# One fused Mamba block with an expert-choice feed-forward on one core: B and C are projected and split in the first stage, one product with C a batch goes to GpSimd, TensorE adds the skip term, and the feed-forward runs one unit earlier

## The reference

```
# attn: a selective scan
delta, Bmat, Cmat = split(xn @ W_deltaBC.T, [64, 80])      # 64 + 16 + 16 columns
delta  = softplus(delta @ W_dt.T + b_dt)                   # [b, 512, 256]
deltaA = exp(delta[..., None] * -exp(A_log))               # [b, 512, 256, 16]
BX     = delta[..., None] * Bmat[:, :, None, :] * xn[..., None]
h_t    = deltaA_t * h_(t-1) + BX_t                         # scan over the 512 tokens
y      = einsum('blds,bls->bld', h, Cmat) + D * xn
# ffn: 8 experts, each takes its 128 best tokens of every batch
G, I = top_k(softmax(xn @ Wg.T over experts), 128)
out  = G * (gelu(xn[I] @ W1 + b1) @ W2 + b2)               # 256 -> 1024 -> 256
ffn  = scatter-add of out at I
```

## Time and profile before

| | |
|---|---|
| median of 3 runs | 2486.82 us |
| the profiled execution | 2487.14 us, of which the span of the trace is 2485.3 us |
| TensorE products busy | 2352.3 us, 95% |
| VectorE busy | 2420.4 us, 97% |
| ScalarE busy | 1971.0 us, 79% |
| GpSimd busy | 2200.9 us, 89% |
| DMA | 325.38 MB, mean 131 GB/s |

### The profile page before, as it was taken

How to read it: one execution, slowest core, us unless ns; L and a number is a source line. 1 busy time by engine, 2 the same in 40 slices (tenths; PEclk the granted TensorE clock), 3 DMA queues, 4 the chain that set the end, 5 groups by cost and what they waited for, 6 DMA issues and landing times. The chain is left out here.

```text
span 2485.3 us, 32917 instructions
## 1 busy us (share of the span) xinstructions
PE 2352.3 (95%) x10524; PEld 1773.3 (71%) x10524; DVE 2420.4 (97%) x2090; ACT 1971.0 (79%) x3432; POOL 2200.9 (89%) x1260
## 2 busy tenths in 40 slices
PE   7829999999999999999999999999999999999996
PEld 3307777777777777777777777777777777777775
DVE  7889999999999999999999999999999999999995
ACT  6627888888888888888888888888888888888783
POOL 4317999999989999999999999999999999999996
PEclk9959999999999999999999999999999999999998
DMA  9762464535444444454545353444544445454433
GB/s 344 254 255 79 129 182 126 145 96 130 118 116 134 116 125 109 116 134 100 151 101 149 91 143 99 132 117 117 135 115 125 110 115 132 100 151 93 106 92 54
DMA packets 162973, 325.38 MB, mean 131 GB/s; under 512 B 16272, under 2 KB 133104, under 8 KB 146160
## 3 DMA queue, kind: packets, MB, share of 16 engines
q1 hardware_dynamic: 95536, 239.11, 28.1%
q0 software_dynamic: 66048, 83.92, 20.2%
q10 hardware_dynamic: 1216, 0.23, 0.0%
HBM read 250.84 MB, written 84.93 MB: 135 GB/s over the span
## 5 line engine op out<-in xcount | busy, mean ns | idle before, releaser
L499 POOL TENSOR_TENSOR ysum<-ysum,prod 128x1024 f32<-128x1024 f32 x480 | 1306.5, 2722 | 32.7 <-DVE prod L909 23.0
L900 DVE TENSOR_TENSOR_SCAN bank_x<-decay,bank_x 128x1024 f32<-128x1024 f32 x512 | 1169.6, 2284 | 0.0
L1106 PE MATMUL bank_l<-ext,w_sb 128*128 128x256 f32 x4096 | 970.2, 382 | 4.3 <-ACT og L693 4.2
L1125 PE MATMUL bank_l<-w_sb,hid 128*128 128x256 f32 x4096 | 957.2, 383 | 0.0
L1125 PEld LDWEIGHTS bank_l<-w_sb,hid 128*128 128x128 f32 x4096 | 762.5, 190 | 164.0 <-issue 67.7
L1106 PEld LDWEIGHTS bank_l<-ext,w_sb 128*128 128x128 f32 x4096 | 756.5, 190 | 141.5 <-issue 23.5
L643 ACT ACTIVATE hid<-bank_l,b_all 128x256 f32<-128x256 f32 x1024 | 431.0, 475 | 339.6 <-PE bank_l L1106 339.1
L634 ACT ACTIVATE decay<-delta,a_sb 128x511 f32<-128x511 f32 x1024 | 640.7, 707 | 4.8 <-POOL delta L462 3.5
L909 DVE TENSOR_TENSOR prod<-bank_x,c_all 128x1024 f32<-128x1024 f32 x512 | 623.0, 1217 | 0.1
L847 DVE TENSOR_TENSOR bank_x<-du,bank_b 128x1024 f32<-128x1024 f32 x512 | 615.7, 1203 | 0.0
L518 POOL DMA_INDIRECT out<-og,idx_all x256 | 408.6, 1596 | 49.4 <-POOL ysum L499 34.5
(11 more groups left out here) (95 smaller groups left out, 1545.9 us busy)
## 6 DMA issues: line engine op xcount, KB each, us to landing
c_all<-c_rows SPq DMA_DIRECT2D x128, 1024.0 KB, 5.4
w_sb<-in_w SPq DMA_DIRECT2D x32, 1024.0 KB, 7.4
decay<-in_x SPq DMA_DIRECT2D x32, 512.0 KB, 6.3
xn_rows<-c_all SPq DMA_DIRECT2D x32, 512.0 KB, 4.9
out<-yrow POOLq DMA_DIRECT2D x32, 512.0 KB, 7.0
xr<-xn_rows SPq DMA_DIRECT2D x30, 512.0 KB, 6.6
ex<-xn_rows,idx_all POOLq DMA_INDIRECT x256, 2.8
out<-og,idx_all POOLq DMA_INDIRECT x256, 4.9
```

Source lines behind the costliest of these rows:

```text
L499: nc.gpsimd.tensor_tensor(ysum[:, m % 2], first, prod[:, i], ALU.add).then_inc(sum_done, 1)
L900: nc.vector.tensor_tensor_scan(bank_x[:, s % 2], decay[:, k % 2, i].rearrange("p c t -> p (c t)"), bank_x[:, s % 2], 0.0, ALU.mult, ALU.ad ...
L1106: i = nc.tensor.matmul(bank_l[(q + k) % 2][:, (f % 2) * UT:(f % 2 + 1) * UT], w1_sb[:, e2, hc, f * P:(f + 1) * P], ext[:, k % 2, hc], star ...
L1125: i = nc.tensor.matmul(o, hid[:, (k - 1) % 2, f, c * K:(c + 1) * K], w2_sb[:, le2, f], start=False, stop=(f == FC - 1 and c == UB - 1))
```

## The change

In the row loop the gate weights and the 96 columns of `W_deltaBC` stand side by side in `wpj_sb` (104 columns), and one product a batch gives logits, delta's low-rank part, B and C. ScalarE copies it out (`proj`), SP stores the 96 rows to the DRAM tensor `bc_rows` and gathers eight batches' B rows (16 each) on 128 partitions in `b_whole`. For each such group the split in three bfloat16 parts is done once (`split_hi`, `split_mid` on ScalarE, `split_rest`, `split_lo` on GpSimd), and the parts go to DRAM (`b_rows`). The main loop reloads what it needs (`load_rank`, `load_b`, `load_c`). `project`, `take_bc`, `take_rest`, `take_mid`, `take_lo` and VectorE's copy of logits are gone. The logits of four batches are turned with 16 small transposes instead of four.

In each batch the step with state 4 (`GP_STEP`) scans into an own tensor `state`, and GpSimd multiplies it by the C row. The first sum of a batch adds the products of states 0 and 1, so there are 15 sums. `skip` is a second operand of TensorE's turning of `ysum` (two transposes that accumulate in the bank). Tokens lie as `(p c)` in a tile instead of `(c p)`, so that a partition's four rows are 4 KB in one piece of DRAM; the turnings write PSUM, or read `ysum` and `skip`, with a stride of four elements. The feed-forward runs a unit earlier: unit 0 goes up before the main loop, unit `u + 1` in unit `u`. The picks of the first half are awaited after the second round, and are turned by TensorE before `expand`.

```diff
+PJ = E + BC
+SPLIT = P // N
+NG = NB // SPLIT
+GP_STEP = 4
-        x_tiles = x.rearrange("b (c p) d -> b p c d", p=P)
+        x_tiles = x.rearrange("b (p c) d -> b p c d", p=P)
...
+            def store_proj(b):
+                held(proj_done, b + 1)
+                sp.dma_start(bc_rows[b], proj[E:PJ, b % 4]).then_inc(proj_out[b % 4], 16)
+                sp.dma_start(b_whole[b % SPLIT * N:b % SPLIT * N + N, b // SPLIT],
+                             proj[E + R:E + R + N, b % 4]).then_inc(proj_out[b % 4], 16)
+            def store_parts(g):
+                for part, done in enumerate((hi_done, mid_done, lo_done)):
+                    held(done, g + 1)
+                    sp.dma_start(b_rows[part, g * P:(g + 1) * P, :], b_parts[:, part, g % 2]).then_inc(parts_out[g % 2], 16)
...
             load_c(0)
+            for g in range(2, NG):
+                store_parts(g)
             for part in range(4, HALF // UB):
                 residual(part)
...
# GpSimd, main loop
-                            pool.wait_ge(prod_done, s + 1)
-                            if n == 0:
-                                pool.wait_ge(skip_done, b + 1)
+                            if n == GP_STEP:
+                                pool.wait_ge(scan_done, s + 1)
+                                pool.wait_ge(c_in[u % 2], (u // 2 + 1) * 16)
+                                wait(pool, sum_done, sums(s - 2))
+                                nc.gpsimd.tensor_tensor(prod[:, i], state[:], c_all[:, u % 2, i][:, None, :].broadcast_to([P, HC, T]),
+                                                        ALU.mult).then_inc(gp_prod_done, 1)
+                                pool.wait_ge(gp_prod_done, b + 1)
+                            else:
+                                pool.wait_ge(prod_done, dve_prods(s + 1))
...
-                            take_rest(b + 2)
-                            take_lo(b + 2)
-                                gather(u + 2)
+                                gather(u + 3)
+                        if i in (1, 2) and there(u - 1, NU) and u < NU:
+                            scatter(u - 1, i - 1)
+                        if i == 2 and u == NU - 1:
+                            scatter(u, 0)
+                            scatter(u, 1)
...
+                        if i == 0 and u == NU:
+                            add_y(NB - 1, NU)
# ScalarE, row loop
+                    if there(b - 3, NB):
+                        act.wait_ge(logits_done, b - 2)
+                        wait(act, proj_out[(r - 3) % 4], (b - 3) // 4 * 32)
+                        wait(act, lg_tr, (b - 3) // GATE)
+                        nc.scalar.copy(proj[:, (r - 3) % 4], lg_banks[(r - 3) % 2][0:PJ, :]).then_inc(proj_done, 1)
# VectorE
-                        nc.vector.tensor_copy(lgt, lg_banks[gp][0:GATE * E, :]).then_inc(lgt_done, 1)
...
+                        if n == GP_STEP:
+                            wait(dve, gp_prod_done, b)
+                            into = state[:].rearrange("p c t -> p (c t)")
+                        else:
+                            into = bank_x[:, s % 2]
...
+                        if n == GP_STEP:
+                            continue
# TensorE
-                                i = nc.tensor.transpose(tr_banks[par][:, hc, c * P:(c + 1) * P],
+                                i = nc.tensor.transpose(tr_banks[par][:, hc, :].rearrange("p (r c) -> p c r", c=TC)[:, c],
                                                         xno[:, r % 4, c, hc * P:(hc + 1) * P], ident[:])
...
-                        o = nc.tensor.transpose(bank_t[:, (c % 2) * D + dt * P:(c % 2) * D + (dt + 1) * P],
-                                                ysum[:, par, dt, c * P:(c + 1) * P], ident[:])
+                        part = bank_t[:, (c % 2) * D + dt * P:(c % 2) * D + (dt + 1) * P]
+                        for term in (ysum, skip):
+                            o = nc.tensor.matmul(part, term[:, par, dt, :].rearrange("p (r c) -> p c r", c=TC)[:, c], ident[:],
+                                                 start=(term is ysum), stop=(term is skip), is_transpose=True)
...
             probs_lines(1, bank_l[1], NB // GATE)
-            project(1, 0, 16)
-            pe.wait_ge(hi_done, 1)
+            picks_lines(0)
             expand(1, 0)
...
+            for q in range(FC // 2):
+                up(0, q)
+            chosen_columns(1, 32, 1)
             picks_lines(1)
```

More of the change, by code:

```diff
@@ L120, in build @@
         zabs = sb("zabs", [P, HC, T])
-        yrow = sb("yrow", [P, TC, D])
-        bc_all = sb("bc_all", [BC, T])
-        bc_hi = sb("bc_hi", [P, T], BF16)
-        bc_mid = sb("bc_mid", [P, T], BF16)
-        bc_lo = sb("bc_lo", [P, T], BF16)
-        bc_rest = sb("bc_rest", [P, T])
+        state = sb("state", [P, HC, T])
+        yrow = sb("yrow", [P, 2, TC, D])
+        rank = sb("rank", [R, T])
+        b_parts = sb("b_parts", [P, 3, 2, T], BF16)
         bcs = sb("bcs", [3 * 2 * N, 2, T], BF16)
@@ L523, in main @@
-                        if i == 3 and sl == 0 and there(b - 2, NB):
-                            y = b - 2
-                            pool.wait_ge(yrow_done, y * 2 + 2)
-                            wait(pool, y_added, 16 * y)
-                            last = [w for w in range(min(u - 1, NU)) for c in range(UB) if batch_of(w, c) == y]
-                            if last:
-                                pool.wait_ge(scattered[last[-1] % 2][y % UB], (last[-1] // 2 + 1) * 16)
-                            y_before[y] = True
-                            pool.dma_start(out_tiles[y], yrow[:], accum_op=ALU.add).then_inc(y_added, 16)
+                            if there(u + 3, NU):
+                                gather(u + 3)
@@ L676, in _ @@
             act.wait_ge(b1_in, 16)
-            act.wait_ge(picks_done, 2)
-            take_ext(0, 1, 0)
+            for pair in range(FC // 2):
+                gelus(0, 0, pair)
+            take_ext(1, 2, 0)
+            split_hi(NG - 1)
+            split_mid(NG - 1)
             def main(j):
@@ L1062, in main @@
                             expand(b + 2, 1)
[L1063 to L1064 removed]
+                        if q == 0 and 0 < b < NB and sl == y_slot(b):
+                            pe.wait_ge(sum_done, sums(b * N))
+                            pe.wait_ge(skip_done, b)
                             y_rows((m - 1) % 2, 0)
```

449 lines of the change are left out of this document (229 added, 220 removed).

## The result

The changed kernel takes 2447.36 us (median of 4 runs, 2446.84 to 2450.41), the kernel before 2486.95 us (4 runs, 2486.71 to 2487.46): ratio 0.9843, 95% interval 0.9826 to 0.9860. So it is faster by 39.6 us, 1.6%; 44.8 were forecast. The profiled execution took 2447.02 us with a span of 2445.2, and is compared here with the one before (span 2485.3).

What follows compares the result with a forecast made beforehand. VectorE was taken to set the main loop. From 2487.14 us, main loop -30.4, row loop and opening -5.2, and tail -9.4 gave 2442.1, forecast as a median of 2442, range 2430 to 2470.

Steps and rivals of the forecast that it cites:

- the price of the dependent pair: Main loop, VectorE: a scan right behind its input's writer costs 0.19 us extra, so a batch gains 0.95 us.
- The same slack: Main loop, TensorE: needs 1.0 us less per batch, batch 0.95 shorter, so its 3.7 us waiting for VectorE stays.
- The pace that TensorE allows: Row loop: TensorE's work allows a batch every 3.3 us after the change, against 3.2 before.
- VectorE's wait, and with it TensorE's gap of 0.85: Row loop: VectorE's 3.15 us wait for logits goes, and with it TensorE's 0.85 us gap per four batches.
- The DMA term: Row loop: 1.28 MB at 382 GB/s make 3.35 us a batch, against 3.09 before.
- the rate of 382 GB/s: Row loop: DMA rate assumed with 4 KB pieces, from residual copies 12% better by share; 340 before.
- the order: Opening: first picks turned ahead of both expands and asked for one round later, removing VectorE's wait: -7.4 us.
- opening starves: Rival, opening: second C load or second picks come late behind store_parts and copies, +5 to +15 us; chance 0.08.
- the half clock: Tail: turnings at half clock, counted only in the low end, 5 us, of the 9.4 us gain.
- The rule of the Trainium skill: Turnings at a 16-byte step: non-contiguous PSUM access slows matmuls much, SBUF reads pay on leaving a 16-byte line.
- a sign that it is wrong: Row and main loop turnings: counterparts of L942 or L1005 taking more than 0.11 us each would show the prediction wrong.
- the rival: Row and main loop: turnings with a step are slow, up to 0.43 us each, 2645 us; chance of losing 0.07.

Runs made afterwards that it cites:

- experiment 1: Changed kernel with GpSimd's product put back on VectorE, the rest of the change kept: 2476.92 us, ratio 0.9958 to the kernel before.
- experiment 6: Kernel before with only the token layout changed to (p c), pieces of 4 KB: 2486.27 us, ratio 0.9996 to the kernel before.
- experiment 4: Changed kernel with the old (c p) layout, pieces of 1 KB and turnings without a step: 2444.79 us, ratio 0.9830 to the kernel before.
- experiment 3: Changed kernel with the first picks turned behind both expands again and awaited one round earlier: 2449.83 us, ratio 0.9849 to the kernel before.

## Why the prediction was right, and where it missed

The limit was read rightly: VectorE sets the main loop before and after, and one product a batch, moved to an engine with just enough room, is most of the gain (28.9 of 39.6 us, experiment 1). The time came 5 us over the forecast, and the parts of the table account for 4.9 of them.

*Main loop, 1.6 short.* The step that failed is the price of the dependent pair. I took 0.19 us, from a scan followed by its product. The pair that arises is another one, input and then scan, and costs 1.34 - 1.11 = 0.23 over the independent start: a step of 3.53 instead of 3.49, 1.3 us over 32 batches. Experiment 1 shows that nothing else in the change bears on the main loop.

*GpSimd* was sized well: 69.1 of 70.1 a batch where I had 68.6, 2363 ns for the product where I had 2365. One reading was wrong without consequence: a scan is done 2.2 us before its product is, and not 3.3, which is from start to start.

*TensorE.* "The same slack" was wrong as a statement about whom it waits for: 117.7 us of waiting for VectorE became 25.9. Experiment 1 divides this. With the product back on VectorE TensorE waits 71.1 us for it, so the rest of the change takes 47 us of this wait away and the product's move 45. The new waits are those for ScalarE's `og` and `hid`, 46.1 and 27.8 us there and 47.1 and 28.2 in the changed kernel, so they come with the rest of the change; which part of it was not tried. It cost nothing, since in no batch VectorE waited for TensorE. Whether a wait for ScalarE can be spent like one for VectorE is not shown.

*Row loop, 2.5 short.* The forecast had two errors that partly hide each other. The pace that TensorE allows was over-priced, 3.3 us a batch; it did 3.04. Sixteen small turnings cost 1.1 us where I had 1.7, and a batch's eight turnings and product take less than 2.86, which no run explains: two batches of those four stand 2.6 us apart, with a step and without one. That VectorE's wait, and with it TensorE's gap of 0.85, would go was right. The DMA term was under-priced, 3.35 us a batch; it was 3.84 in the ten batches behind 53 us. The failed step is the rate of 382 GB/s, taken from the residual copies. These ran at 397 with another size, direction and company, and the trace did not say which of these did it. The pieces alone gave 7% by share in experiment 6 and 2% in experiment 4, not 12. At the old 347 the same 1.28 MB give 3.7, and that is near what came. That the numbering came 4.7 us later and not 0.66 (3.84 less before's 12.72 / 4 = 3.18) for each of the batches left fits VectorE's rounds, which pace the end of the row loop.

*Opening.* The sum of -7.4 was right. Its reason, the order, was not the only one at work: without it 4.3 of the 7.4 would have gone with `project` (experiment 3). The rival "opening starves" did not come. The second picks are read at 181.68 without idle time, behind the numbering and the first input, and TensorE stood ready for them 5.1 us before the numbering, where I had 7.

*Tail, 0.7 short.* The last sum ended where I had it. Sixteen turnings at the lower clock, 1.7 us for eight instead of 1.2, and the steps between them and the addition make up the 1.7 us by which the addition is later than forecast; the addition itself was 1.0 shorter. I had put the half clock into the range and not into the value. The row of before at 2454.11 is from a stretch in which TensorE was at work. Before's trace has another one behind an idle time, at the lower clock, and it takes nearly twice as long for the same four turnings:

```profile
2470.79 1.11 PE L1005 MATMUL bank_t<-ident,ysum 128*128 128x128 f32 x4 [5.43 <-ACT yrow L593]
```

The shorter addition is in part the pieces' work: with 1 KB it takes 7.7 us to the span's end (experiment 4) instead of 7.1. Before, two additions and four scatters stood behind the last sum, and each addition and the scatters next to it waited for one another's landing: 5.61 us for the first addition's, then 2.86 for the last scatters'.

*The rule of the Trainium skill* on non-contiguous access, page "SBUF — State Buffer", section "Door 1: The DMA port swizzle": for writing PSUM this case does not bear it out. Turnings with a step of 16 bytes (L1004) and without take 1.09 us for eight alike: with it here, without it before and in experiment 4. For reading SBUF it shows a little. Loading `ysum` or `skip` as weights with that step takes a median of 209 and 211 ns, where L1005 of before took 141:

```profile
L1059 PEld LDWEIGHTS bank_t<-ident,ysum x256: 195/209/231, 303.9 to 2436.3; 128*128 128x128 f32 x128
```

```profile
L1005 PEld LDWEIGHTS bank_t<-ident,ysum x256: 137/141/230, 308.3 to 2471.3; 128*128 128x128 f32 x128
```

Experiment 4, without the step, has 140 and 141 again. The turnings of `ysum` and `skip` follow one another at 0.12 us instead of 0.11. By the letter of the prediction, more than 0.11 was a sign that it is wrong; but sixteen turnings a batch at 0.01 more are 0.2 us (an estimate) on an engine that is not the limit, and 0.12 is far from the 0.28 at which the rival would have turned the sign.

*Open.* Why 4 KB pieces moved less than 1 KB pieces in the changed row loop, with more gaps, although they cost the engines less time. That the DMA engines themselves are the limit there is not shown: their share is 0.98, where the kernels with 1 KB reach 1.04 and 1.06. Loads, stores of `xn`, stores of `proj` and single rows of `b_whole` share SP's queue, and their mix was not taken apart.

## What to carry to other kernels

Moving one instruction a batch from a full engine to one that is nearly full paid here once and would not have paid twice, so work out the need of both per period, not their busy share, and double the moved work as an experiment to see how much room is left. Price a new dependent pair by the same pair, and a rate by transfers of the same kind and company: neighbours that look alike were off by a fifth and by a tenth here. At the end of a kernel, put what nobody waits for behind what the last result waits for, and price TensorE there at its lower clock, since it came out of idle time here.

## What the runs showed of the hardware that was not expected

- Writing PSUM with a step of four elements cost a turning nothing (1.09 us for eight either way), and loading weights with that step took 209 ns instead of 141.
- Pieces of 4 KB gave 348 GB/s and pieces of 1 KB 363 in the same stretch of the same kernel, though at its start, without gaps, 4 KB gave 415 and 1 KB 390; in the kernel before, 343 at a share of 0.94 and 347 at 1.02.
- A product with a row broadcast over eight blocks cost GpSimd what one with two full operands cost: 2363 and 2365 ns.
- The DMA rate was no constant of the stretch: 347 GB/s grew to 367 when 0.23 MB a batch more were there to store.
